# Graph network with 16 channels: TensorE gathers 28 and 31 of each super's 64 tiles, where it gathered 23 and 24

## The chip, the cores and the metric

The kernel runs on one core of a Trainium2 chip. The metric is the device time of one execution in microseconds, lower is better. The engines are TensorE (PE in the rows; PEld is its weight load), VectorE (DVE), ScalarE (ACT), GpSimd (POOL) and SyncE (SP, which only issues DMAs here).

## The reference

12500 nodes with 16 channels, 400000 edges sorted by destination. Two rounds of message passing with the same edge network, then a residual and a layer norm:

```python
w = relu(edgefeats @ fnet_w1 + fnet_b1) @ fnet_w2 + fnet_b2      # 13 -> 32 -> 16*16 per edge
W = w.reshape(-1, 16, 16)
inv_deg = 1.0 / maximum(segment_sum(ones, edge_dst), 1.0)
for _ in range(2):
    xj = hx[edge_src]                                            # gather of 16 floats per edge
    m = einsum('ei,eio->eo', xj, W)
    agg = segment_sum(m, edge_dst) * inv_deg[:, None]
    hx = gru_cell(agg, hx, ...)
out = layernorm(x + hx)
```

## The kernel before

**Tiling.** A tile is 128 edges. 64 tiles make a super, and there are 49 supers (the last one is short). A super is worked through in 8 halves `k` of 8 tiles each (`HPS = 8`, `HT = 8`). Two rounds go over all supers; between them and behind the second stand the GRU cell and the norm. Pairs of supers are the body of loops (`for_supers`); the order of instructions on each engine is the order of the code, and engines meet at semaphores.

**Two ways to gather.** The source rows of a tile, 128 rows of 16 floats, reach `xg` in one of two ways. GpSimd issues an indirect DMA for the tile (L535, waiting at each half until the products of `LEAD = 4` halves earlier are done). Or TensorE makes them: the whole node table lies in SBUF as `parts` (two parts of the floats, 125 partitions, 4 blocks of 400 columns); ScalarE builds a one-hot matrix from the tile's keys (`src_hots`: four ACTIVATE Abs at L603, one ACTIVATE Relu at L607 over all of them, for all such tiles of a half together), TensorE multiplies it with the table in 8 matmuls of 400 columns (`gather_rows`, L722: 4 blocks times 2 parts) into a PSUM bank, VectorE masks the 25 candidate rows (`pick_rows`, L1137, one instruction a tile) and sums them (`keep_rows`, L1145, one a half). `BY_PE[rnd][k]` says how many of a half's 8 tiles TensorE makes: 2, then seven times 3 in round 0 (23 of 64), eight times 3 in round 1 (24 of 64). The first super of a round is gathered by GpSimd alone. The tiles that TensorE makes in super `s` belong to super `s + 1`.

**Buffers.** `ps_g` has three PSUM banks (3, 6, 5), one for each tile of a half, and a tile waits until the same bank's last tile has been picked (`slot_free`). The first layer `hidden` (L709, round 0 only, for the next super) uses bank 2 and waits until ScalarE's relu has read it. The keys of a super are loaded by one DMA of 768 KB (L452), in a ring of two.

**TensorE's order in one half** (`emit`, L792): `products` (L732, waits for VectorE's `fan`), in round 0 `hidden`, then at `k` = 0, 2, 4, 5, 6 sums of the super before (`own_sums` L745, `aggregate` L755, `turn` L762, `scatter` L776), then `gather_rows` of the half's tiles. A fp32 matmul of the code is two MATMULs in the rows; one of the gathers is one.

**ScalarE's order**: `src_hots` of half `k + 1` stands ahead of `keep_products` (L576) and `relu` (L570) of half `k`. **VectorE's order**: `spread` (L1092), the next one-hot (L1080), `keep_hot` (L1100), sums of windows, then the picks of half `k - 1` and their sum. **SP's order** in one super: `idx`, `ef`, `keys`, `h_d` or `h_sb`, each behind its wait.

Of the kernel before, what the change touches and what calls it, by code (L numbers as in the profile page):

```python
# [10 lines left out]
ALU = mybir.AluOpType  # L11
# [21 lines left out]
BY_PE = ((2, 3, 3, 3, 3, 3, 3, 3), (3, 3, 3, 3, 3, 3, 3, 3))  # L33
# [4 lines left out]
TG = sum(GT)  # L38
PARTS = 2
# [14 lines left out]
def gnn_program(nc, x, x_t, src_tiles, src_pe_rows, src_pe_cols, dst_rows, dst_tiles, ef_t, w1_diag, w2_io, w2_oi,  # L54
# [77 lines left out]
    with ExitStack() as ctx:  # L132
# [6 lines left out]
        def sem(name):  # L139
# [31 lines left out]
        shared = sb("shared", [P, 4320 + 3 * C * AR])  # L171
# [3 lines left out]
        near_tmp, far_tmp = (shared[:, lo:lo + CHUNK * TPB] for lo in (3920, 4120))  # L175
        picked = shared[:, 4320:4320 + 3 * C * AR].rearrange("p (m c a) -> p m c a", m=3, a=AR)
# [3 lines left out]
        place = sb("place", [GROUP, 2 * BPS, SPAN])  # L180
# [5 lines left out]
        m_of, h_of = mh[:, 0:GN], mh[:, GN:2 * GN]  # L186
        h_x = sb("h_x", [P, HA])
        x_x = sb("x_x", [P, C])
        rel_x = sb("rel_x", [P, 1])
        h_xt = sb("h_xt", [HA, P])  # L190
        prod_x = sb("prod_x", [P, C, C])
        msg_x = sb("msg_x", [P, CNT + 1])
        hot_x = sb("hot_x", [P, XWIN])
        keys = sb("keys", [P, 2, TG * P], I16)
# [45 lines left out]
        ps_g = [ps_all[:, b * BANK:b * BANK + AR * C] for b in (3, 6, 5)]  # L240
# [315 lines left out]
        def _(act):  # L556
# [34 lines left out]
            def src_hots(rnd, i, par, s, k):  # L591


                buf, use = ring(rnd, i, par)
                first, some = sum(GT[:k + 1]) - BY_PE[rnd][k], BY_PE[rnd][k]
                if k == 0:
                    act.wait_ge(s_keys[buf], 16 * keys_use(rnd, i, par))
# [102 lines left out]
        def _(pe):  # L700
            pe.wait_ge(s_net, 16 * NET_LOADS)

            def hidden(rnd, i, par, sup, k):
# [734 lines left out]
```

## Time and profile before

| what | value |
|---|---|
| median of 3 runs | 5147.61 us (5144.84 to 5148.1) |
| span of the profiled execution | 6694.6 us |
| TensorE matmul busy | 5648.0 us, 84% |
| weight load busy | 4666.6 us, 70% |
| VectorE busy | 4296.9 us, 64% |
| GpSimd busy | 3811.1 us, 57% |
| ScalarE busy | 3179.0 us, 47% |
| chain that ended last | PE 65%, issue 14%, another core or an unknown queue 10%, ACT 6%, DVE 3% |

The profiled execution is 1547 us longer than the median of the runs without a profile. Its span can't be compared with the median directly. VectorE's `place<-` instruction (L1151) runs once a super, at `k = 2`, and serves as a clock of the supers.

### The profile page before, as it was taken

Reading aid. Unit: us, or ns where it says so; the run is one execution under the profiler, and the core shown is the slowest. Engines: PE = TensorE matmul, PEld = TensorE weight load, DVE = VectorE, ACT = ScalarE, POOL = GpSimd, SP = SyncE. Lnnn points to the kernel's source line nnn. Section 1 sums busy time; section 2 is a strip of 40 time slices with the busy share of each in tenths; the row PEclk is TensorE's granted clock in tenths of the full one; section 3 lists DMA queues with packets and bytes.
Section 4 is the critical chain, followed back from the end, with each engine's and each line's share of the span. In section 5 each row is a group of like instructions: output and inputs, shape, how many; then the busy total and the mean of one; then the engine's idle time right before and its main releaser. Section 6 shows DMA issues by size and latency. Waiting matters only on the chain.

```text
span 6694.6 us, 119595 instructions
## 1 busy us (share of the span) xinstructions
PE 5648.0 (84%) x38360; PEld 4666.6 (70%) x38361; DVE 4296.9 (64%) x7146; ACT 3179.0 (47%) x5259; POOL 3811.1 (57%) x4021
## 2 busy tenths in 40 slices
PE   2888888888888888888858888888888888888887
PEld 1777777777777777777647777776777777777775
DVE  3766666666666666666636666666666666666665
ACT  1554555445554545454325454454545454444442
POOL 6355555555555555555555555555555555555553
PEclk7988998889898999998878898898988889888887
DMA  4111111111111111111111111111111111111110
GB/s 107 46 34 48 34 48 34 48 34 48 34 48 44 39 48 34 48 34 48 25 47 29 40 29 40 33 37 39 31 40 29 40 29 41 29 40 29 40 29 20
DMA packets 197656, 263.32 MB, mean 39 GB/s; under 512 B 95745, under 2 KB 165942, under 8 KB 184205
## 3 DMA queue, kind: packets, MB, share of 16 engines
q1 hardware_dynamic: 61885, 216.66, 9.5%
q0 software_dynamic: 128192, 33.07, 4.8%
q10 hardware_dynamic: 7026, 6.21, 0.4%
q8 instruction: 348, 5.70, 0.4%
q14 instruction: 205, 1.68, 0.1%
HBM read 195.73 MB, written 54.92 MB: 37 GB/s over the span
## 4 chain that ended last, share of the span: by engine, by line
PE 65%; issue 14%; another core or an unknown queue 10%; ACT 6%; DVE 3%; DVEq 1%; DMA 0%; POOL 0%; ACTq 0%; POOLq 0%; SPq 0%
PE ps_all L722 45%; PE ps_all L732 8%; ACT src_hot L603 3%; PE ps_all L755 3%; PE ps_all L745 3%; PE ps_all L709 3%; PE ps_all L776 2%; ACT src_hot L607 2%; DVE shared L1137 1%; DVE fan L1092 1%; PE ps_all L762 0%; ACT shared L576 0%; ACT h_sb L570 0%; DVE xg L1145 0%
## 5 line engine op out<-in xcount | busy, mean ns | idle before, releaser
L722 PE MATMUL ps_all<-parts,src_hot 125*128 125x400 f32 x18048 | 3820.4, 368 | 258.7 <-issue 166.4
L722 PEld LDWEIGHTS ps_all<-parts,src_hot 125*128 125x128 f32 x18048 | 3501.9, 202 | 482.6 <-issue 367.7
L535 POOL DMA_INDIRECT xg<-in_x,idx x2027 | 1923.4, 949 | 1394.3 <-issue 556.1
L535 POOL DMA_INDIRECT xg<-h_rows,idx x1979 | 1873.1, 946 | 1371.6 <-issue 518.7
L1137 DVE TENSOR_TENSOR shared<-ps_all,at_hot 128x400 f32<-128x400 f32 x2256 | 1211.8, 566 | 1858.8 <-remote 1168.4
L603 ACT ACTIVATE src_hot<-keys,neg_key 128x384 fp32r<-128x384 int16 (+1 forms) x3072 | 1617.0, 599 | 1653.1 <-remote 979.0
L732 PE MATMUL ps_all<-fan,h_sb 128*32 128x160 f32 x12544 | 825.0, 316 | 489.5 <-issue 435.8
L1092 DVE TENSOR_TENSOR fan<-xg,ps_all 128x1280 f32<-128x1280 f32 x784 | 1158.8, 1478 | 88.0 <-DVE xg L1145 33.4
L607 ACT ACTIVATE src_hot<-src_hot 128x1536 fp32r<-128x1536 f32 (+1 forms) x768 | 1122.2, 1461 | 72.3 <-ACT src_hot L603 2.8
L1145 DVE TENSOR_REDUCE xg<-shared 128x48 f32<-128x1200 f32 (+1 forms) x768 | 1056.7, 1376 | 75.6 <-DVE shared L1137 1.0
L732 PEld LDWEIGHTS ps_all<-fan,h_sb 128*32 128x32 f32 x12544 | 391.8, 111 | 842.4 <-issue 794.9
L576 ACT COPY shared<-ps_all 128x320 f32<-128x320 f32 x784 | 330.2, 421 | 638.1 <-remote 431.2
L582 ACT COPY agg_sb<-ps_all 128x160 f32<-128x160 f32 x98 | 28.7, 293 | 981.0 <-remote 630.7
L755 PE MATMUL ps_all<-shared,w2s 128*64 128x160 f32 x3136 | 328.9, 349 | 70.3 <-issue 69.3
L745 PE MATMUL ps_all<-xg,shared 128*80 128x136 f32 (+1 forms) x1568 | 323.0, 317 | 75.1 <-issue 58.7
L709 PE MATMUL ps_all<-w_sb,ef 105*128 105x264 f32 x784 | 314.5, 483 | 66.5 <-issue 43.9
L745 PEld LDWEIGHTS ps_all<-xg,shared 128*80 128x80 f32 x1568 | 223.5, 168 | 193.1 <-issue 150.3
L755 PEld LDWEIGHTS ps_all<-shared,w2s 128*64 128x64 f32 x3136 | 259.3, 161 | 126.5 <-issue 117.6
L1165 DVE TENSOR_TENSOR acc_all<-acc_all,ps_all 33x144 f32 (+1 forms) x384 | 114.1, 297 | 236.3 <-remote 174.3
L709 PEld LDWEIGHTS ps_all<-w_sb,ef 105*128 105x128 f32 x784 | 131.0, 207 | 191.1 <-issue 179.4
L776 PE MATMUL ps_all<-place,agg_t 80*33 80x144 f32 (+1 forms) x1568 | 189.6, 336 | 64.0 <-issue 60.4
L1115 DVE TENSOR_TENSOR shared<-ps_all,mask 80x256 f32<-80x256 f32 (+3 forms) x490 | 180.4, 368 | 42.1 <-remote 20.4
(120 smaller groups left out, 1383.7 us busy)
## 6 DMA issues: line engine op xcount, KB each, us to landing
keys<-key_d SPq DMA_DIRECT2D x96, 768.0 KB
h_d<-h_sb SPq DMA_DIRECT2D x49, 1056.0 KB
h_sb<-h_d SPq DMA_DIRECT2D x49, 1056.0 KB
xg<-in_x,idx POOLq DMA_INDIRECT x2027
xg<-h_rows,idx POOLq DMA_INDIRECT x1979
ef<-in_ef_t SPq DMA_DIRECT2D x49, 420.0 KB
acc_all<-agg_t SPq DMA_DIRECT2D x1, 3161.0 KB
idx<-in_src_tiles SPq DMA_DIRECT2D x98, 32.0 KB
```

Source lines behind the costliest of these rows:

```text
L535: pool.indirect_dma_start(out=xg[:, buf, at, 0:C], out_offset=None, in_=rows_of, in_offset=bass.IndirectOffsetOnAxis(ap=idx[:, buf, at:at ...
L576: act.copy(pev[:, :, 2 * k:2 * k + 2, :].rearrange("p i u n -> p u i n"), ps_p[k % 2][:, 0:2 * C * WIN].rearrange("p (u i n) -> p u i n", ...
L603: act.activation(src_hot[:, k % 2, kb, 0:some * P], keys[:, buf, first * P:(first + some) * P], ACT.Abs, bias=neg_key[:, kb:kb + 1]).then_ ...
L607: act.activation(hot_of, hot_of.bitcast(F32), ACT.Relu, bias=1.0, scale=-1.0).then_inc(s_src_hot, some)
L709: pe.matmul(ps_h[:, 0:HT * HA], ef[:, buf, k, :], w1_sb[:], start=True, stop=True).then_inc(s_h, 1)
L722: last = pe.matmul(ps_g[j], src_hot[0:KP, k % 2, kb, j * P:(j + 1) * P], parts[0:KP, m, kb, :], start=(kb == 0 and m == 0), stop=(kb == KB ...
L732: last = pe.matmul(ps_p[k % 2][b * HID:(b + 1) * HID, u * C * WIN:(u + 1) * C * WIN], h_sb[:, buf, k * HT + u * BPS + b, 0:HID], fan[:, k ...
L745: last = pe.matmul(ps_own[n][:, u, 0:TQ * ca], hot_sb[:, j, b].rearrange("p t n -> p (t n)"), xg[:, buf].rearrange("p (j t b) c -> p j b t ...
L755: last = pe.matmul(ps_agg[lo:lo + BPS * C, 0:TPB * WIN], w2s[:, i, :], pev[:, i].rearrange("p t n -> p (t n)"), start=(i < 2), stop=(i >= ...
L1092: dve.tensor_tensor(fan[:, k % 2], xg[:, buf, k * HT:(k + 1) * HT, 0:C].unsqueeze(3).to_broadcast([P, HT, C, WIN]), hot[:, k % 2].unsqueez ...
L1137: dve.tensor_tensor(picked[:, j], ps_g[j].rearrange("p (a c) -> p c a", a=AR), at_hot[:, u].unsqueeze(1).to_broadcast([P, C, AR]), ALU.mul ...
L1145: dve.tensor_reduce(xg[:, buf, at:at + many, 0:C], picked[:, 0:many], AX_X, ALU.add).then_inc(s_xg_pe, many)
```

## The change

`BY_PE` becomes 3, 3, 4, 3, 3, 4, 4, 4 in round 0 (28 tiles) and 3, then seven times 4 in round 1 (31 tiles). A fourth tile of a half has its own place in `ps_g`, which is bank 2, that of the first layer. In round 0 the first layer of the next super therefore moves behind the half's first gathered tile, waits until the last fourth tile has been picked, and the fourth tile waits until the relu of this half has read the bank. Keys are loaded by two DMAs a super (halves 0 to 3 and 4 to 7, two single buffers in place of a ring of two), and the first of them stands ahead of the `idx` load in SP's queue. `place` moves into `mh`, the scratch of rare tiles and of the setup into one tile `rare`, to make room.

```diff
-BY_PE = ((2, 3, 3, 3, 3, 3, 3, 3), (3, 3, 3, 3, 3, 3, 3, 3))
+BY_PE = ((3, 3, 4, 3, 3, 4, 4, 4), (3, 4, 4, 4, 4, 4, 4, 4))
+KQ = HPS // 2
+GQ = (sum(GT[:KQ]), sum(GT[KQ:]))
...
+    def fourth_before(rnd, k):
+        back = next(b for b in range(1, HPS + 1) if BY_PE[rnd][k - b] > 3)
+        return sum(BY_PE[rnd][:k - back]) + 3 - (0 if k >= back else sum(BY_PE[rnd]))
...
-        ps_g = [ps_all[:, b * BANK:b * BANK + AR * C] for b in (3, 6, 5)]
+        ps_g = [ps_all[:, b * BANK:b * BANK + AR * C] for b in (3, 6, 5, 2)]
...
+                def keys_of(rnd, i, par, q):
+                    sup = 2 * i + par
+                    made = sum(BY_PE[rnd][:KQ * (q + 1)])
+                    wait_pos(sp, s_src_hot, pe_total(rnd) if is_first(i, par) else pe_count(rnd, sup, made))
+                    sp.dma_start(keys[:, q, 0:GQ[q] * P], ...).then_inc(s_keys[q], 16)
...
+                    if not is_last(i) and not (is_first(i, par) and rnd == 0):
+                        keys_of(rnd, i, par, 0)
                     wait_pos(sp, s_super, done)
                     sp.dma_start(idx[:, buf, :], src_tiles[bass.ds(sup * P, P), :]).then_inc(s_idx[buf], 16)
...
                     if not is_last(i):
-                        wait_pos(sp, s_src_hot, pe_total(rnd) if is_first(i, par) else pe_count(rnd, sup, 0))
-                        sp.dma_start(keys[:, 1 - buf, :], ...)
+                        keys_of(rnd, i, par, 1)
...
-            def hidden(rnd, i, par, sup, k):
+            def hidden(rnd, i, par, sup, k, s=None):
...
+                if s is not None:
+                    free = fourth_before(rnd, k)
+                    if not (isinstance(s, int) and s == 1 and free < 0):
+                        pe.wait_ge(s_picked, pe_count(rnd, s, free) + 1)
...
+                    if j == 3 and rnd == 0:
+                        pe.wait_ge(s_relu, sup * HPS + k + 1)
...
-                        if rnd == 0 and not is_last(i):
-                            hidden(rnd, i + par, 1 - par, sup + 1, k)
...
-                            gather_rows(rnd, s + 1, k)
+                            gather_rows(rnd, s + 1, k, (0,))
+                            if rnd == 0:
+                                hidden(rnd, i + par, 1 - par, sup + 1, k, s + 1)
+                            gather_rows(rnd, s + 1, k, (1, 2, 3), sup + 1)
...
-                                pick_rows(rnd, s + 1, k - 1, (2,))
+                                pick_rows(rnd, s + 1, k - 1, (2, 3))
```

TensorE, round 0, halves 5 and 6 of a super, before (L709 is the first layer, L722 the gathers, L732 the products):

```order
L732 MATMUL ps_all<-fan,h_sb 32x160 x8
L709 MATMUL ps_all<-w_sb,ef 128x264
L745 MATMUL ps_all<-xg,shared 80x136
L776 MATMUL ps_all<-place,agg_t 33x144 x4
L722 MATMUL ps_all<-parts,src_hot 128x400 x24
L732 MATMUL ps_all<-fan,h_sb 32x160 x8
L709 MATMUL ps_all<-w_sb,ef 128x264
L745 MATMUL ps_all<-xg,shared 80x136 x2
L722 MATMUL ps_all<-parts,src_hot 128x400 x24
```

The same halves in the changed kernel, where L727 is the first layer, L744 the gathers and L754 the products:

```order
L754 MATMUL ps_all<-fan,h_sb 32x160 x8
L767 MATMUL ps_all<-xg,shared 80x136
L798 MATMUL ps_all<-mh,agg_t 33x144 x4
L744 MATMUL ps_all<-parts,src_hot 128x400 x8
L727 MATMUL ps_all<-w_sb,ef 128x264
L744 MATMUL ps_all<-parts,src_hot 128x400 x24
L754 MATMUL ps_all<-fan,h_sb 32x160 x8
L767 MATMUL ps_all<-xg,shared 80x136 x2
L744 MATMUL ps_all<-parts,src_hot 128x400 x8
L727 MATMUL ps_all<-w_sb,ef 128x264
L744 MATMUL ps_all<-parts,src_hot 128x400 x24
```

Each of these halves has 32 gather matmuls in place of 24, and the first layer stands between the first 8 and the rest.

SP's queue in round 0, one super in the loop, before:

```order
L431 ISA [waits s_super]
L431 DMA idx<-in_src_tiles 128x64
L402 REGISTER_ALU
L441 ISA [waits s_h]
L441 DMA ef<-in_ef_t 105x1024
L402 REGISTER_ALU
L452 ISA [waits s_src_hot]
L452 DMA keys<-key_d 128x3072
L459 ISA [waits s_relu]
L459 DMA h_d<-h_sb 128x2112
```

And in the changed kernel:

```order
L435 ISA [waits s_src_hot]
L435 DMA keys<-key_d 128x1920
L446 ISA [waits s_super]
L446 DMA idx<-in_src_tiles 128x64
L406 REGISTER_ALU
L456 ISA [waits s_h]
L456 DMA ef<-in_ef_t 105x1024
L406 REGISTER_ALU
L435 ISA [waits s_src_hot]
L435 DMA keys<-key_d 128x2048
L473 ISA [waits s_relu]
L473 DMA h_d<-h_sb 128x2112
```

The load of the first half's keys, with a wait of its own, now stands ahead of `idx`; the second stands where the whole load stood.

## Rows read from the trace of the kernel before

**Rows 1.** VectorE's timeline, one row a super: start us, us, instruction.

```profile
215.06 1.35 DVE L1151 TENSOR_TENSOR place<-ps_all,slot_of 80x1152 f32<-80x1152 f32 x1
...
3305.59 1.34 DVE L1151 TENSOR_TENSOR place<-ps_all,slot_of 80x1152 f32<-80x1152 f32 x1
...
3528.01 1.34 DVE L1151 TENSOR_TENSOR place<-ps_all,slot_of 80x1152 f32<-80x1152 f32 x1
...
6608.58 1.34 DVE L1151 TENSOR_TENSOR place<-ps_all,slot_of 80x1152 f32<-80x1152 f32 x1
```

**Rows 2.** TensorE's timeline, round 1, halves 4 to 6 of a super.

```profile
4333.19 0.45 PE L745 MATMUL ps_all<-xg,shared 128*80 128x128 f32 x2
4333.57 0.68 PE L776 MATMUL ps_all<-place,agg_t 80*32 80x144 f32 x8
4334.18 4.64 PE L722 MATMUL ps_all<-parts,src_hot 125*128 125x400 f32 x24
4338.75 0.75 PE L732 MATMUL ps_all<-fan,h_sb 128*32 128x160 f32 x16
4339.43 0.67 PE L745 MATMUL ps_all<-xg,shared 128*80 128x128 f32 x4
4339.86 4.62 PE L722 MATMUL ps_all<-parts,src_hot 125*128 125x400 f32 x24
4344.41 0.75 PE L732 MATMUL ps_all<-fan,h_sb 128*32 128x160 f32 x16
```

**Rows 3.** TensorE's timeline, round 0: halves 2 and 3; and half 0, two tiles.

```profile
3039.63 3.19 PE L722 MATMUL ps_all<-parts,src_hot 125*128 125x400 f32 x16
3042.74 0.75 PE L732 MATMUL ps_all<-fan,h_sb 128*32 128x160 f32 x16
...
3052.79 0.71 PE L709 MATMUL ps_all<-w_sb,ef 105*128 105x264 f32 x2
3053.34 0.63 PE L745 MATMUL ps_all<-xg,shared 128*80 128x136 f32 x4
3053.81 0.43 PE L762 MATMUL ps_all<-fold,agg_sb 128*80 128x64 f32 x4
3054.05 4.62 PE L722 MATMUL ps_all<-parts,src_hot 125*128 125x400 f32 x24
...
3059.28 0.71 PE L709 MATMUL ps_all<-w_sb,ef 105*128 105x264 f32 x2
3059.63 4.54 PE L722 MATMUL ps_all<-parts,src_hot 125*128 125x400 f32 x23
```

**Rows 4.** TensorE's timeline, start of a super in round 1: single products with idle time between.

```profile
4356.23 0.47 PE L732 MATMUL ps_all<-fan,h_sb 128*32 128x160 f32 x1 [0.28 <-issue]
...
4358.68 3.03 PE L755 MATMUL ps_all<-shared,w2s 128*64 128x160 f32 x32
4361.64 4.64 PE L722 MATMUL ps_all<-parts,src_hot 125*128 125x400 f32 x24
...
5005.55 0.30 PE L732 MATMUL ps_all<-fan,h_sb 128*32 128x160 f32 x1 [1.78 <-issue]
```

**Rows 5.** GpSimd's timeline, round 1: idle time before each and what ended it.

```profile
4002.78 0.95 POOL L535 DMA_INDIRECT xg<-h_rows,idx  x1 [3.38 <-PE ps_all L732]
4004.04 0.95 POOL L535 DMA_INDIRECT xg<-h_rows,idx  x1 [0.30 <-issue]
4005.29 0.95 POOL L535 DMA_INDIRECT xg<-h_rows,idx  x1 [0.30 <-issue]
```

**Rows 6.** ScalarE's timeline, a half of two tiles and one of three.

```profile
3027.67 1.70 ACT L603 ACTIVATE src_hot<-keys,neg_key 128x256 fp32r<-128x256 int16 x4
3029.47 1.06 ACT L607 ACTIVATE src_hot<-src_hot 128x1024 fp32r<-128x1024 f32 x1
...
3042.32 2.13 ACT L603 ACTIVATE src_hot<-keys,neg_key 128x384 fp32r<-128x384 int16 x4
3044.54 1.48 ACT L607 ACTIVATE src_hot<-src_hot 128x1536 fp32r<-128x1536 f32 x1
```

**Rows 7.** VectorE, busy time and counts of two stretches of 47 supers (windows; PE, PEld, DVE, ACT, POOL in turn).

```profile
215.00:3305.60 3090.60, 2706.68 (x18535) 2248.69 (x18538) 2016.41 (x3351) 1559.30 (x2703) 1807.00 (x1911) 0.91 0.16 41
3528.00:6608.60 3080.60, 2653.66 (x18166) 2218.86 (x18168) 2041.91 (x3377) 1489.93 (x2332) 1773.21 (x1876) 0.88 0.13 35
```

More of the change, by code:

```diff
@@ L107, in landed @@
         return i * (16 * usual) + 16 * (earlier + usual + first + last)
-    def keys_use(rnd, i, par):
-        buf, use = ring(rnd, i, par)
-        return use - sum(ring(r, 0, 0)[0] == buf for r in range(rnd + 1))
     def pe_total(rnd):
@@ L170, in gnn_program @@
         fan = sb("fan", [P, 2, HT, C, WIN])
-        shared = sb("shared", [P, 4320 + 3 * C * AR])
+        shared = sb("shared", [P, 3920 + max(GT) * C * AR])
         pev = shared[:, 0:C * TPB * WIN].rearrange("p (i t n) -> p i t n", i=C, n=WIN)
@@ L174, in gnn_program @@
         own = shared[0:GROUP, 3640:3640 + 2 * CA * TQ]
-        near_tmp, far_tmp = (shared[:, lo:lo + CHUNK * TPB] for lo in (3920, 4120))
-        picked = shared[:, 4320:4320 + 3 * C * AR].rearrange("p (m c a) -> p m c a", m=3, a=AR)
+        picked = shared[:, 3920:3920 + max(GT) * C * AR].rearrange("p (m c a) -> p m c a", m=max(GT), a=AR)
         agg_sb = sb("agg_sb", [P, TPB * WIN])
@@ L179, in gnn_program @@
         slot_of = sb("slot_of", [GROUP, NSUP * 2 * BPS])
-        place = sb("place", [GROUP, 2 * BPS, SPAN])
         acc_all = sb("acc_all", [P, N + SPAN])
@@ L186, in gnn_program @@
         m_of, h_of = mh[:, 0:GN], mh[:, GN:2 * GN]
+        place = mh[0:GROUP, 0:2 * BPS * SPAN].rearrange("g (b n) -> g b n", n=SPAN)
         h_x = sb("h_x", [P, HA])
@@ L189, in gnn_program @@
         rel_x = sb("rel_x", [P, 1])
-        h_xt = sb("h_xt", [HA, P])
-        prod_x = sb("prod_x", [P, C, C])
+        rare = sb("rare", [P, WC + XWIN + P])
+        prod_x = rare[:, 0:WC].rearrange("p (o i) -> p o i", o=C)
+        hot_x = rare[:, WC:WC + XWIN]
+        h_xt = rare[0:HA, WC + XWIN:WC + XWIN + P]
+        near_tmp, far_tmp = (rare[:, lo:lo + CHUNK * TPB] for lo in (0, CHUNK * TPB))
         msg_x = sb("msg_x", [P, CNT + 1])
-        hot_x = sb("hot_x", [P, XWIN])
-        keys = sb("keys", [P, 2, TG * P], I16)
+        keys = sb("keys", [P, 2, max(GQ) * P], I16)
         at_pe = sb("at_pe", [P, NSUP * TG])
@@ L425, in _ @@
             for rnd in range(ROUNDS):
+                def keys_of(rnd, i, par, q):
+                    sup = 2 * i + par
+                    made = sum(BY_PE[rnd][:KQ * (q + 1)])
+                    wait_pos(sp, s_src_hot, pe_total(rnd) if is_first(i, par) else pe_count(rnd, sup, made))
+                    sp.dma_start(keys[:, q, 0:GQ[q] * P],
+                                 key_d[bass.ds(sup + 1, 1), sum(GQ[:q]) * P:sum(GQ[:q + 1]) * P].to_broadcast(
+                                     [P, GQ[q] * P])).then_inc(s_keys[q], 16)
                 def emit(i, par, rnd=rnd):
@@ L449, in emit @@
                         sp.wait_ge(s_key_d, 16)
+                    if is_first(i, par) and rnd == 0:
+                        keys_of(rnd, i, par, 0)
                     if not is_last(i):
-                        wait_pos(sp, s_src_hot, pe_total(rnd) if is_first(i, par) else pe_count(rnd, sup, 0))
-                        sp.dma_start(keys[:, 1 - buf, :],
-                                     key_d[bass.ds(sup + 1, 1), :].to_broadcast([P, TG * P])).then_inc(
-                                         s_keys[1 - buf], 16)
+                        keys_of(rnd, i, par, 1)
                     if rnd == 0 and isinstance(i, int) and i == 0 and par == 1:
@@ L591, in src_hots @@
             def src_hots(rnd, i, par, s, k):
[L594 to L597, printed above, removed]
+                q = k // KQ
+                first, some = sum(GT[KQ * q:k + 1]) - BY_PE[rnd][k], BY_PE[rnd][k]
+                if k % KQ == 0:
+                    act.wait_ge(s_keys[q], 16 * (rnd * (NSUP - 1) + s))
                 if k > 1:
@@ L602, in src_hots @@
                 for kb in range(KB):
-                    act.activation(src_hot[:, k % 2, kb, 0:some * P], keys[:, buf, first * P:(first + some) * P],
+                    act.activation(src_hot[:, k % 2, kb, 0:some * P], keys[:, q, first * P:(first + some) * P],
                                    ACT.Abs, bias=neg_key[:, kb:kb + 1]).then_inc(s_src_far, 1)
@@ L708, in hidden, with gather_rows @@
                 wait_pos(pe, s_relu, sup * HPS + k)
+                if s is not None:
+                    free = fourth_before(rnd, k)
+                    if not (isinstance(s, int) and s == 1 and free < 0):
+                        pe.wait_ge(s_picked, pe_count(rnd, s, free) + 1)
                 pe.matmul(ps_h[:, 0:HT * HA], ef[:, buf, k, :], w1_sb[:],
                           start=True, stop=True).then_inc(s_h, 1)
-            def gather_rows(rnd, s, k):
+            def gather_rows(rnd, s, k, js, sup=None):
                 for j, (n, _, _) in enumerate(pe_tiles(rnd, k)):
+                    if j not in js:
+                        continue
                     pe.wait_ge(s_src_hot, pe_count(rnd, s, n) + 1)
+                    if j == 3 and rnd == 0:
+                        pe.wait_ge(s_relu, sup * HPS + k + 1)
                     if isinstance(s, int) and s == 1 and slot_free(rnd, k, j) < 0:
@@ L844, in emit @@
                                     pe.wait_ge(s_ht_x, tiles_x)
-                                    pe.matmul(ps_x[:, P:P + WC], h_xt[:], w2_sb[:],
+                                    pe.matmul(ps_x[:, P:P + WC], h_xt, w2_sb[:],
                                               start=True, stop=True).then_inc(s_w_x, 1)
@@ L849, in emit @@
                                         pe.wait_ge(s_hot_x, sums_x)
-                                        pe.matmul(ps_x[0:CNT + 1, P + WC:P + WC + XWIN], msg_x[:], hot_x[:],
+                                        pe.matmul(ps_x[0:CNT + 1, P + WC:P + WC + XWIN], msg_x[:], hot_x,
                                                   start=True, stop=True).then_inc(s_sum_x, 1)
@@ L1150, in places @@
                 wait_pos(dve, s_sc, 2 * sup)
-                dve.tensor_tensor(place[:], iota_ps[0:GROUP].unsqueeze(1).to_broadcast([GROUP, 2 * BPS, SPAN]),
+                dve.tensor_tensor(place, iota_ps[0:GROUP].unsqueeze(1).to_broadcast([GROUP, 2 * BPS, SPAN]),
                                   slot_of[:, bass.ds(s * 2 * BPS, 2 * BPS)].unsqueeze(2).to_broadcast(
@@ L1241, in emit @@
                                     dve.wait_ge(s_turn_x, tiles_x)
-                                    dve.tensor_copy(h_xt[:], ps_x[0:HA, 0:P])
+                                    dve.tensor_copy(h_xt, ps_x[0:HA, 0:P])
                                     dve.drain().then_inc(s_ht_x, 1)
@@ L1254, in emit @@
                                         dve.drain()
-                                        dve.tensor_tensor(hot_x[:], iota[:, 0:XWIN],
+                                        dve.tensor_tensor(hot_x, iota[:, 0:XWIN],
                                                           rel_x[:].to_broadcast([P, XWIN]), ALU.is_equal)
```

8 lines of the change are left out of this document (4 added, 4 removed).

## The prediction

> **What bounds the kernel now.** I read the clock of the supers first. Between the `place` rows of the first and the 48th super lie 3305.6 - 215.1 = 3090.5 us in round 0 and 6608.6 - 3528.0 = 3080.6 us in round 1 [rows 1]: 47 supers each, 65.8 and 65.5 us a super. Everything else (setup, the first super of a round, GRU, norm) is 6694.6 - 6171.1 = 523.5 us.
>
> Then I put this against the median, 5147.6 us. If the 523.5 us are the same without a profile, a pair of supers (one of each round) takes (5147.6 - 523.5) / 47 = 98.4 us there, against 131.3 in the trace. So the trace holds some 33 us a pair that the timed runs don't have. TensorE's timeline shows where: at the start of supers, and once more inside them, products run one by one with 0.28 to 1.8 us idle before each, ended by "issue" [rows 4], while in clean stretches all 16 take 0.68 us together [rows 2]. The durations inside clean stretches are what I build on, not the gaps.
>
> TensorE's work of a super, from start to start in clean stretches:
> - gathers of three tiles: 4338.75 - 4334.18 = 4.57 and 4344.41 - 4339.86 = 4.55 us [rows 2]; of two, 3.11 us [rows 3]. One more tile is 1.45 us (8 matmuls of 181 ns).
> - products 0.68 us a half, 5.4 us a super [rows 2]
> - own sums 0.38 us ahead of each of two scatters, 0.43 once [rows 2], 0.47 twice [rows 3]: 2.1 us; scatters 2 x 0.61 = 1.2 us [rows 2]; turn 0.24 us [rows 3]; aggregate 4361.64 - 4358.68 = 2.96 us [rows 4]
> - first layer, round 0 only: 0.55 us in the five halves where sums follow, 0.35 us in three [rows 3]: 3.8 us
>
> Round 1: 8 x 4.56 + 12.0 = 48.5 us. Round 0: 7 x 4.56 + 3.11 + 12.0 + 3.8 = 50.8 us. A pair is 99.3 us, and 523.5 + 47 x 99.3 = 5191 us, 0.8% above the median. So **TensorE, without a gap, accounts for the whole time**. GpSimd accounts for it nearly as well: one indirect DMA starts every 1.25 us [rows 5], 41 and 40 a super are 51.3 and 50.0 us, 101.3 us a pair, 3% above the 98.4. Both engines are full, and in the trace it is GpSimd that waits, for L732 [rows 5].
>
> **The change part by part.**
>
> *Five and seven more tiles on TensorE.* 12 x 1.45 = 17.4 us a pair. Nothing hides it: it stands in TensorE's own queue. 47 x 17.4 = **818 us**. Round 0 is then 58.1 us, round 1 58.7 us, a pair 116.7 us.
>
> *Five and seven fewer on GpSimd.* 36 and 33 a super: 45.0 and 41.3 us. It leaves the path and gives nothing while TensorE needs 58 us. In the first super of a round GpSimd still makes all 64 tiles, 80 us, and covers TensorE's extra tiles there, so 47 supers pay, not 48.
>
> *ScalarE.* Going from two to three tiles, the four Abs go from 1.70 to 2.13 us and the Relu from 1.06 to 1.48 us [rows 6], so four tiles are about 2.56 + 1.90 us, with copy and relu some 5.3 us a half, beside TensorE's 6.0 + 0.7 us or more. Hidden, except at half 1 of a super: its one-hots are only begun when ScalarE has copied the aggregate and the products, and TensorE has by then only one half's gathers and a product ahead. In round 1 half 1 gets a fourth tile, 0.85 us more there; between 0 (slack takes it) and 0.85 x 47 = 40 us. I take 19 us.
>
> *VectorE.* It is busy 2016 / 47 = 42.9 and 2042 / 47 = 43.4 us a super [rows 7]. A tile adds one pick and a third of a three-tile sum, about 1.0 us: 48 and 51 us, under 58. The longer `at_hot` adds 0.2. Hidden; if TensorE's tile were cheaper, this would be the next bound.
>
> *The first layer between gathers, round 0.* Its matmuls are the same. But the gathers are cut once more: 24 matmuls at 181 ns are 4.35 us, the row is 4.56, so each run of gathers has a 0.2 us edge. Eight more edges a super in round 0: 0 (the edge of the first layer may have been paid before) to 8 x 0.19 x 47 = 71 us; I take half, 36 us. Its new wait, the last fourth tile picked, is met: VectorE picks it about 0.6 us after the gather ends, TensorE comes there after products and a tile, over 2 us later. The fourth tile's wait for the relu is closer. ScalarE is free 4.5 us after the last gather ended, plus 0.8 us: 5.3 us; TensorE arrives after 0.68 + 3 x 1.45 + 0.35 = 5.4 us. At worst some 0.3 us in four halves, within the range.
>
> *Keys in two loads, the first ahead of `idx`.* The same bytes and one more issue a super. SP now holds `idx` back until the one-hots of half 3 are made, about when TensorE is in half 2 or 3; behind it are queued `ef`, the second keys and `h_d` or `h_sb`. GpSimd wants `idx` at half 4, and has 58 - 45 = 13 us of slack. The first keys are needed again some four halves later, 28 us. I cost it at nothing; if the cover is gone, one half (7 us) every super, 650 us, which nothing in the order points to. `place` and the scratch move without new work.
>
> Sum against the median: 5147.6 + 818 + 36 + 19 = **6020 us**. A profiled execution has gaps on top: 6694.6 + 870, about 7570 us.
>
> One rule speaks against this. Rows 2 show 4.57 us for 24 matmuls of 400 columns, 190 ns each with the edge. The Trainium skill, TensorE: Matmul & The Clock Gate, "Back-to-back issue gap", gives a stream of weight load and matmul pairs about 81 ns a matmul at 128 columns and 131 at 512. An estimate from that page is 116 ns at 400 columns, a tile 0.93 us, and by it TensorE's pair of supers would be about 86 us and the change would pay: that is the last rival below with the page's price. The trace does not agree with it.
>
> **The rivals.**
>
> *Cheaper gathers than traced, slower all the same: about 5675 us.* A matmul of 400 columns at 2.4 GHz can't take under 167 ns; 181 is 14 more, and those could be the profile's. A tile would be 1.33 us, the pair 116.7 - 59 x 0.12 = 109.6 us, 523.5 + 47 x 109.6 = 5675 us. Before, GpSimd would then have been the bound. For it: both engines account for the median. Against it: 181 ns is steady through every clean run, also right behind idle time.
>
> *A ring of waits takes over: about 6175 us.* Gather, pick, bank free, gather; or relu late for the fourth tile. 0.3 us in each of the 11 four-tile halves of a pair is 47 x 3.3 = 155 us more. For it: ScalarE's 5.3 against 5.4 us. Against: VectorE has 7 us of slack a super.
>
> *The other side, faster: GpSimd is the bound and TensorE has much air in timed runs.* If the issue gaps are the visible part of a slowing that touches every TensorE instruction in the profile, the clean rows overstate it. GpSimd then takes 98.4 / 81 = 1.215 us a tile, and 69 tiles a pair instead of 81 give 83.8 us: 523.5 + 47 x 83.8 = 4460 us at the most favourable, 4460 to 5137 in all. It decides from the point where TensorE's 116.7 us are really under 98.4, 16% less than the rows. Against it: 59 tiles at the columns' own 1.33 us are already 78.7 us, which leaves 19.7 us for edges and work that the rows put at 31. By the page's figure it would come to about 4580 us.
>
> *The change doesn't do what it says*: excluded, the order shows 32 matmuls where 24 stood.
>
> **How the numbers follow.** TensorE full as traced 0.53 (6020, own range 5950 to 6090); cheaper gathers 0.19; ring of waits 0.09; faster 0.16; within 0.2%, which is about what a measurement of this kernel can tell from no change, 0.03. Slower is 0.81. The range 5500 to 6180 us holds the first, nearly all of the second and most of the third, 0.8.
>
> **What would show it.** The changed kernel's clean stretches should show 32 gather matmuls in 6.0 us, the round-0 first layer between 8 and 16 or 24 of them, and GpSimd waiting for L754 in nearly every half, 10 us or more a super. Supers should be 8 us longer in round 0 and 10 in round 1 than before. Wrong would be: gathers at under 170 ns, or GpSimd without waits for the products; and a time near or under 5150 us would say that TensorE was not the bound at all.

## The result and the profile after

| | before | after |
|---|---|---|
| median | 5146.26 us (5144.84 to 5148.1, 4 runs) | 5905.53 us (5902.23 to 5906.21, 4 runs) |
| span of the profiled execution | 6694.6 us | 5904.2 us |

The ratio is 1.1476, 95% interval 1.1462 to 1.149: the change makes the kernel 759 us slower. The profiled execution of the changed kernel is as long as its timed ones. That of the kernel before was 1548 us longer than its timed ones. The experiments show that such a difference goes with the chip that the program runs on; the chip of that first profile isn't on record.

The page of the changed kernel, busy time and what ended most of the idle time (groups: count, busy us, mean ns, idle us before and what ended most of it):

```profile
PE 5698.3 (97%) x42968; PEld 5092.0 (86%) x42969; DVE 4856.4 (82%) x7722; ACT 3663.0 (62%) x5259; POOL 3261.6 (55%) x3445
...
L744 PE MATMUL ps_all<-parts,src_hot 125*128 125x400 f32 x22656 | 4467.0, 351 | 30.1 <-ACT src_hot L621 23.2
...
L549 POOL DMA_INDIRECT xg<-in_x,idx x1787 | 1696.2, 949 | 1211.2 <-PE ps_all L754 739.1
L549 POOL DMA_INDIRECT xg<-h_rows,idx x1643 | 1550.8, 944 | 1324.9 <-PE ps_all L754 920.3
```

TensorE is 97% busy. GpSimd, with 576 indirect DMAs fewer, waits for the products 1659 us in all, and TensorE waits for ScalarE's one-hots only 23 us. TensorE's timeline in round 1, halves 3 to 5, the pendant of [rows 2]:

```profile
4020.82 0.75 PE L754 MATMUL ps_all<-fan,h_sb 128*32 128x160 f32 x16
4021.50 6.10 PE L744 MATMUL ps_all<-parts,src_hot 125*128 125x400 f32 x32
4027.53 0.75 PE L754 MATMUL ps_all<-fan,h_sb 128*32 128x160 f32 x16
4028.21 0.45 PE L767 MATMUL ps_all<-xg,shared 128*80 128x128 f32 x2
4028.59 0.69 PE L798 MATMUL ps_all<-mh,agg_t 80*32 80x144 f32 x8
4029.20 6.09 PE L744 MATMUL ps_all<-parts,src_hot 125*128 125x400 f32 x32
4035.23 0.75 PE L754 MATMUL ps_all<-fan,h_sb 128*32 128x160 f32 x16
```

Four tiles take 4027.53 - 4021.50 = 6.03 us, 1.46 us more than the 4.57 of three [rows 2], with nothing between the groups. Round 0, one half with the first layer inside the gathers, between its products and the next ones, the pendant of [rows 3]:

```profile
2010.60 0.75 PE L754 MATMUL ps_all<-fan,h_sb 128*32 128x160 f32 x16
2011.28 1.72 PE L744 MATMUL ps_all<-parts,src_hot 125*128 125x400 f32 x8
2012.84 0.61 PE L727 MATMUL ps_all<-w_sb,ef 105*128 105x264 f32 x2
2013.09 4.72 PE L744 MATMUL ps_all<-parts,src_hot 125*128 125x400 f32 x24
2017.73 0.75 PE L754 MATMUL ps_all<-fan,h_sb 128*32 128x160 f32 x16
```

The clock of the supers, VectorE's `place` instruction (now in `mh`, L1174), as in [rows 1]:

```profile
174.13 1.35 DVE L1174 TENSOR_TENSOR mh<-ps_all,slot_of 80x1152 f32<-80x1152 f32 x1
...
2898.61 1.34 DVE L1174 TENSOR_TENSOR mh<-ps_all,slot_of 80x1152 f32<-80x1152 f32 x1
...
3084.08 1.34 DVE L1174 TENSOR_TENSOR mh<-ps_all,slot_of 80x1152 f32<-80x1152 f32 x1
...
5825.98 1.34 DVE L1174 TENSOR_TENSOR mh<-ps_all,slot_of 80x1152 f32<-80x1152 f32 x1
```

47 supers take 2724.5 and 2741.9 us: 57.97 and 58.34 us each, 116.3 a pair. The forecast had 58.1 and 58.7 plus 1.2 for edges and waits.

### The profile page after: what moved, and what is told of

It is laid out like the page before. It is cut to its first block, busy times and chain, and to the rows that moved or that the text cites. A ratio compares the mean times of both kernels' runs of the same rounds, so it can differ in the third digit from the quotient of the medians.

```text
span 5904.2 us, 131764 instructions
## 1 busy us (share of the span) xinstructions
PE 5698.3 (97%) x42968; PEld 5092.0 (86%) x42969; DVE 4856.4 (82%) x7722; ACT 3663.0 (62%) x5259; POOL 3261.6 (55%) x3445
## 4 chain that ended last, share of the span: by engine, by line
PE 89%; ACT 3%; issue 3%; DVE 2%; DMA 2%; POOL 1%; DVEq 0%; SPq 0%; POOLq 0%; ACTq 0%
PE ps_all L744 67%; PE ps_all L754 8%; PE ps_all L767 4%; PE ps_all L777 4%; PE ps_all L727 3%; PE ps_all L798 2%; ACT src_hot L617 2%; POOL xg L549 1%; ACT src_hot L621 1%; DMA acc_all<-agg_t 1%; PE ps_all L784 0%; DMA h_sb<-h_d 0%; PE ps_all L930 0%; DVE fan L1115 0%; DVE shared L1160 0%
## 5 line engine op out<-in xcount | busy, mean ns | idle before, releaser
L744 PE MATMUL ps_all<-parts,src_hot 125*128 125x400 f32 x22656 | 4467.0, 351 | 30.1 <-ACT src_hot L621 23.2
L744 PEld LDWEIGHTS ps_all<-parts,src_hot 125*128 125x128 f32 x22656 | 4084.4, 188 | 198.9 <-issue 116.4
L617 ACT ACTIVATE src_hot<-keys,neg_key 128x512 fp32r<-128x512 int16 (+1 forms) x3072 | 1862.5, 678 | 1016.2 <-PE ps_all L744 1004.0
L549 POOL DMA_INDIRECT xg<-in_x,idx x1787 | 1696.2, 949 | 1211.2 <-PE ps_all L754 739.1
L549 POOL DMA_INDIRECT xg<-h_rows,idx x1643 | 1550.8, 944 | 1324.9 <-PE ps_all L754 920.3
L1160 DVE TENSOR_TENSOR shared<-ps_all,at_hot 128x400 f32<-128x400 f32 x2832 | 1527.0, 566 | 674.5 <-PE ps_all L744 656.5
L621 ACT ACTIVATE src_hot<-src_hot 128x2048 fp32r<-128x2048 f32 (+1 forms) x768 | 1369.8, 1784 | 70.5
L1168 DVE TENSOR_REDUCE xg<-shared 128x64 f32<-128x1600 f32 (+1 forms) x768 | 1297.3, 1689 | 81.1 <-DVE shared L1160 2.4
L754 PE MATMUL ps_all<-fan,h_sb 128*32 128x160 f32 x12544 | 599.4, 309 | 115.2 <-DVE fan L1115 103.8
L754 PEld LDWEIGHTS ps_all<-fan,h_sb 128*32 128x32 f32 x12544 | 331.5, 110 | 335.3 <-issue 283.7
L727 PE MATMUL ps_all<-w_sb,ef 105*128 105x264 f32 x784 | 244.1, 392 | 30.9 <-DMA ef<-in_ef_t 18.8
L777 PEld LDWEIGHTS ps_all<-shared,w2s 128*64 128x64 f32 x3136 | 213.3, 141 | 19.5 <-issue 17.4
L1103 DVE TENSOR_TENSOR ps_all<-ps_all,rel 128x80 f32<-128x80 f32 x784 | 189.3, 241 | 0.2 <-DVE ps_all L1092 0.2
```

What stands on the lines that cost most here:

```text
L549: pool.indirect_dma_start(out=xg[:, buf, at, 0:C], out_offset=None, in_=rows_of, in_offset=bass.IndirectOffsetOnAxis(ap=idx[:, buf, at:at ...
L617: act.activation(src_hot[:, k % 2, kb, 0:some * P], keys[:, q, first * P:(first + some) * P], ACT.Abs, bias=neg_key[:, kb:kb + 1]).then_in ...
L621: act.activation(hot_of, hot_of.bitcast(F32), ACT.Relu, bias=1.0, scale=-1.0).then_inc(s_src_hot, some)
L727: pe.matmul(ps_h[:, 0:HT * HA], ef[:, buf, k, :], w1_sb[:], start=True, stop=True).then_inc(s_h, 1)
L744: last = pe.matmul(ps_g[j], src_hot[0:KP, k % 2, kb, j * P:(j + 1) * P], parts[0:KP, m, kb, :], start=(kb == 0 and m == 0), stop=(kb == KB ...
L754: last = pe.matmul(ps_p[k % 2][b * HID:(b + 1) * HID, u * C * WIN:(u + 1) * C * WIN], h_sb[:, buf, k * HT + u * BPS + b, 0:HID], fan[:, k ...
```

## The experiments

Three jobs ran on chips where the kernel before takes 5145 us, two on chips where the same program takes 6712 and 6742 us in all its runs. I call them chips without gaps and with gaps. A time below is compared only with the kernel before of its own job.

**1. The kernel before again.** No edit.

> The kernel before, unchanged, profiled once more. Its first profiled execution was 6694.6 us long against 5146 us timed, with idle time ended by issue in front of TensorE's small matmuls; the changed kernel's profiled execution (5904.2 us) had none. If the profile of this kernel makes the gaps, the span is 6600 to 6800 us again and the time 5146. If they were an accident of that one execution, the span is about 5145 us, the supers are about 50.1 us each, and GpSimd's waits for the products can be read.

Measured: 6737.75 us; the kernel before took 6742.34 us there (19 timed runs, 6695 to 6774), profiled span 6744.8. Neither expectation was met in full: the gaps are neither the profile's nor an accident, and on this chip the kernel takes 1600 us more, timed or profiled. TensorE's timeline there:

```profile
4299.23 0.31 PE L732 MATMUL ps_all<-fan,h_sb 128*32 128x160 f32 x1 [0.98 <-issue]
4299.95 0.30 PE L732 MATMUL ps_all<-fan,h_sb 128*32 128x160 f32 x1 [0.41 <-issue]
4301.35 0.47 PE L732 MATMUL ps_all<-fan,h_sb 128*32 128x160 f32 x2 [1.11 <-issue]
4302.07 0.43 PE L732 MATMUL ps_all<-fan,h_sb 128*32 128x160 f32 x1 [0.24 <-issue]
4303.47 0.76 PE L732 MATMUL ps_all<-fan,h_sb 128*32 128x160 f32 x3 [0.97 <-issue]
```

The starts are 0.72 and 1.40 us apart where sixteen should take 0.68 us, and no semaphore ends the waits.

The granted clock of TensorE belongs to this picture: its mean is 0.880 here and 0.981 in experiment 9, on a chip without gaps. When the burst above begins the clock is still full (1.00 up to 4300 us); from 4302 to 4308 us it is at its lower level (0.50, 1.2 GHz), and the 24 gather matmuls behind the burst take 5.45 us in place of 4.57. Over the whole run the clock is at the lower level for 1616 us in 176 stretches, against 199 us in 22 stretches in experiment 9; 148 of the 176 begin within 3 us of such a gap. So the 1587 us between the two profiles (6744.8 - 5158.0) are idle time and low clock together: TensorE's matmuls are busy 5653.5 us here and 4914.0 us there, for the same 38360 instructions.

**2. The structure of the change with the old table.**

```diff
-BY_PE = ((3, 3, 4, 3, 3, 4, 4, 4), (3, 4, 4, 4, 4, 4, 4, 4))
+BY_PE = ((2, 3, 3, 3, 3, 3, 3, 3), (3, 3, 3, 3, 3, 3, 3, 3))
```

> The changed kernel with the table of before (23 and 24 tiles): keys in two halves ahead of idx, the first layer behind the first gathered tile, scratch moved; the tile counts alone undone. If the tiles on TensorE are the whole cost, as forecast, the time is 5146 us plus the forecast's edges of 36 us at most, 5130 to 5185. If the keys ahead of idx or the moved first layer cost something of their own, it is 5200 or more, and the tiles cost less than 1.45 us each.

Beside the table, `fourth_before` returns nothing when a round has no fourth tile, and `shared` keeps its size. The waits between the first layer and the fourth tile are therefore absent here.

Measured: 6720.72 us against 6742.34, ratio 0.9977 (0.9953 to 1.0001), on the chip with gaps. The structure alone costs nothing visible there. For a chip without gaps it says little, as what bounds the kernel isn't the same.

**3 and 4. Half of the gather matmuls.** Both kernels leave out the low part of the nodes in the gathers, so their gathered rows are rounded.

```diff
-                        for m in range(PARTS):
+                        for m in range(1):
...
-                                             start=(kb == 0 and m == 0), stop=(kb == KB - 1 and m == PARTS - 1))
+                                             start=(kb == 0 and m == 0), stop=(kb == KB - 1))
```

> The kernel before with the low part of the nodes left out of the gathers (4 matmuls a tile in place of 8, so the gathered rows are rounded). TensorE's pair of supers falls from about 98.3 us in clean rows to 98.3 - 47 x 0.73 = 64 us. If GpSimd sets the time of the kernel before (81 tiles x 1.25 us = 101.3 us a pair), nothing is gained: 5100 to 5146 us. If TensorE sets it and GpSimd has air, the time falls by a good part of the 34 us a pair: under 4800 us.

> The changed kernel with the low part of the nodes left out of the gathers (4 matmuls a tile in place of 8). TensorE's pair falls from 116.3 to about 116.3 - 59 x 0.73 = 73 us. What is next then sets the time: GpSimd's 69 tiles x 1.25 = 86.3 us a pair give about 438 + 47 x 86.3 = 4490 us; VectorE's 48 + 51 us busy give about 5090 us. Either way far under 5905: the added matmuls are the cost.

Measured, on the chip with gaps: 6440.24 us (ratio 0.9549) and 5978.44 us (ratio 0.8853), the kernel before at 6742.34. Half of the gather matmuls gone gives 302 us in the kernel before, though 18048 / 2 matmuls at 181 ns are 1633 us. That isn't the price of the matmuls on such a chip: the mean granted clock fell with them, from 0.880 in experiment 1 to 0.786, and a gather matmul's mean duration rose from 370 to 415 ns. The expectations were made for a chip without gaps, so they stay untested, and so does the question of the bound there; experiments 7, 9 and 10 settle it.

**5. The changed kernel again.** No edit; a chip without gaps.

> The changed kernel, unchanged. In the runs before this one the kernel before took 6742 us on its chip, with the issue gaps of its first profile, timed or profiled alike, so the gaps come with the chip and not with the profile. If this chip is free of them, the kernel before takes 5146 us and this one 5905. If it has them, the kernel before takes 6742 us. Theory 1 (the gaps come after runs of small matmuls that empty TensorE's queue, and longer gathers refill it): this one is then slower by less than on the good chip, 6742 plus 0 to 400 us. Theory 2 (a fixed loss of some 15 us a super): 6742 + 760 = 7500 us.

Measured: 5903.81 us against 5144.58, ratio 1.1478 (1.1459 to 1.1497): the result repeats.

**6. A table between the two**, on the structure of the change (here too `fourth_before` may return nothing, which doesn't come up with this table):

```diff
-BY_PE = ((3, 3, 4, 3, 3, 4, 4, 4), (3, 4, 4, 4, 4, 4, 4, 4))
+BY_PE = ((3, 3, 3, 3, 3, 3, 4, 3), (3, 3, 4, 3, 3, 4, 3, 3))
```

> The changed kernel with 25 and 26 tiles a super on TensorE, between the two tables. On a chip without gaps TensorE is full from 98.3 us a pair on: 98.3 + 4 x 1.45 = 104.1 us a pair, 438 + 47 x 104.1 = 5331 us. If GpSimd set the time of the kernel before, with TensorE having air, it is below 5146. On a chip with gaps: between the two kernels' own times there.

Measured: 5400.39 us against 5144.58, ratio 1.0497 (1.048 to 1.0515). Slower than both expectations, with 25 and 26 tiles; supers of 53.7 and 51.9 us. Three and five tiles of 1.45 us fewer than 57.97 and 58.34 would be 53.6 and 51.1: round 0 is as the tiles say, round 1 0.8 us over. The trace has these 0.8 us (waiting line, waited for: us in total, times, longest us):

```profile
PE ps_all L756 <- DMA h_sb<-h_d: 35.6, 43, 1.6
```

35.6 us over 47 supers are 0.76 us each. TensorE waits for the nodes' load, which stands behind the second key load in SP's queue. With the kernel before (experiments 9 and 10) this wait doesn't appear, and in the changed kernel's profile it is 1.3 us in all. So with shorter supers the new order of the loads seems to have a price; no run with the old order and this table shows it apart.

**7. Fewer tiles on TensorE**, on the kernel before:

```diff
-BY_PE = ((2, 3, 3, 3, 3, 3, 3, 3), (3, 3, 3, 3, 3, 3, 3, 3))
+BY_PE = ((2, 3, 2, 3, 3, 2, 3, 3), (3, 3, 2, 3, 3, 2, 3, 3))
```

> The kernel before with 21 and 22 tiles a super on TensorE in place of 23 and 24. On a chip without gaps: if GpSimd sets the time of the kernel before (1.25 us a tile), a pair is 85 x 1.25 = 106.3 us and the time 438 + 47 x 106.3 = 5430 us, some 5 us per super slower. If TensorE sets it alone and GpSimd has air, 4 x 1.45 us less a pair: 5146 - 270 = 4876 us. On a chip with gaps GpSimd waits for TensorE, so fewer tiles are faster or the same, 6500 to 6742 us.

Measured: 5385.35 us against 5144.58, ratio 1.0467 (1.0449 to 1.0484). Fewer tiles are slower: GpSimd sets the time. The waits of this kernel (engine, line, waited for: us in total, times, longest us):

```profile
DVE fan L1092 <- DMA xg<-h_rows,idx: 504.1, 271, 17.8
DVE fan L1092 <- DMA xg<-in_x,idx: 485.9, 236, 5.7
...
POOL xg L535 <- PE ps_all L732: 48.8, 160, 0.3
```

VectorE waits 990 us for landings of the indirect DMAs, and GpSimd waits for nobody: 160 waits of at most 0.3 us are the usual pause between two DMAs. The 5385 us are 45 under the expected 5430.

**8. The first layer ahead of the first gathered tile**, on the changed kernel, round 0:

```diff
-                            gather_rows(rnd, s + 1, k, (0,))
                             if rnd == 0:
                                 hidden(rnd, i + par, 1 - par, sup + 1, k, s + 1)
+                            gather_rows(rnd, s + 1, k, (0,))
```

> The changed kernel with the first layer ahead of the half's first gathered tile in round 0, as before the change; it still waits for the last fourth tile's pick. The forecast put 0 to 71 us on the cut of the gathers, 36 taken. The rows of the changed kernel put it at nothing: the two edges of a cut half are 0.17 us each more, the first layer's own time 0.25 us in place of 0.35 to 0.55. So by the forecast it is 36 us faster than 5905 on a chip without gaps, by the rows within 10 us; slower by more than 30 us if the earlier place makes TensorE wait for VectorE's pick of the fourth tile.

Measured: 5892.63 us, 11 us under the 5903.81 of the same job. Between the two expectations, nearer to the rows.

**9. The kernel before on a chip without gaps.** No edit.

> The kernel before once more, for its profile on a chip without gaps. With 21 and 22 tiles GpSimd issued an indirect DMA every 1.249 us through both rounds without a pause, and 4198 x 1.249 us plus 138 us around them are its 5384 us. The kernel before has 4006: 4006 x 1.249 + 138 = 5141 us. If GpSimd sets its time, the profile shows it waiting for the products for less than 50 us in all and the products waiting for fan. If TensorE sets it (47 pairs x 98.3 us in clean rows plus about 438 around them: 5058 us), GpSimd waits for the products in most halves. On a chip with gaps: 6742 us, as there.

Measured: 5144.94 us, ratio 1.0; profiled span 5158.0. The waits:

```profile
DVE fan L1092 <- DMA xg<-h_rows,idx: 293.0, 181, 17.4
...
POOL xg L535 <- PE ps_all L732: 67.5, 210, 2.3
```

GpSimd's timeline there, and TensorE's a little later:

```profile
4004.83 0.94 POOL L535 DMA_INDIRECT xg<-h_rows,idx  x1 [0.30 <-PE ps_all L732]
4006.08 0.95 POOL L535 DMA_INDIRECT xg<-h_rows,idx  x1 [0.30 <-issue]
```

```profile
4005.15 2.39 PE L755 MATMUL ps_all<-shared,w2s 128*64 128x160 f32 x32
4007.47 4.64 PE L722 MATMUL ps_all<-parts,src_hot 125*128 125x400 f32 x24
4012.86 0.75 PE L732 MATMUL ps_all<-fan,h_sb 128*32 128x160 f32 x16 [0.75 <-DVE fan L1092]
...
4031.28 4.64 PE L722 MATMUL ps_all<-parts,src_hot 125*128 125x400 f32 x24
4036.73 0.75 PE L732 MATMUL ps_all<-fan,h_sb 128*32 128x160 f32 x16 [0.80 <-DVE fan L1092]
```

GpSimd's waits put down to the products, 67.5 us in 210 times, are mostly the usual 0.3 us between two DMAs (210 x 0.3 = 63). It keeps its 1.25 us, and TensorE is the one that waits, 0.75 and 0.80 us for `fan`. The clock of the supers:

```profile
128.48 1.35 DVE L1151 TENSOR_TENSOR place<-ps_all,slot_of 80x1152 f32<-80x1152 f32 x1
...
2529.17 1.34 DVE L1151 TENSOR_TENSOR place<-ps_all,slot_of 80x1152 f32<-80x1152 f32 x1
...
2719.72 1.34 DVE L1151 TENSOR_TENSOR place<-ps_all,slot_of 80x1152 f32<-80x1152 f32 x1
...
5067.49 1.34 DVE L1151 TENSOR_TENSOR place<-ps_all,slot_of 80x1152 f32<-80x1152 f32 x1
```

2400.7 and 2347.8 us for 47 supers are 51.08 and 49.95 us a super; 41 and 40 DMAs at 1.249 us are 51.2 and 50.0. In these stretches GpSimd issues 1916 and 1877 indirect DMAs, 1.251 us apart in the mean; only 9 and none of them start more than 1.3 us after the one before. The kernel before runs at GpSimd's pace.

**10. One tile more than before.**

```diff
-BY_PE = ((2, 3, 3, 3, 3, 3, 3, 3), (3, 3, 3, 3, 3, 3, 3, 3))
+BY_PE = ((3, 3, 3, 3, 3, 3, 3, 3), (3, 3, 3, 3, 3, 3, 3, 3))
```

> The kernel before with 24 tiles in both rounds, three in every half. If GpSimd sets the time, 48 indirect DMAs fewer are 48 x 1.249 = 60 us off it, and TensorE gets 48 x 1.45 = 70 us more: 438 + 47 x 99.8 = 5129 us is its own sum, GpSimd's is 5081. So 5129 us or a little under 5144 if the two meet there; 5190 or more if TensorE was the bound before.

Measured: 5194.34 us against 5145.35, ratio 1.0097 (1.008 to 1.0114). The expectation of 5129 was wrong, and by its number 5190 should mean that TensorE was the bound before. Experiments 7 and 9 exclude that. Round 0 went from 51.1 to 52.1 us a super where GpSimd's 40 DMAs need 50.0: with the 24th tile TensorE has crossed over. The 5129 us rested on a sum of clean rows of 50.1 us for 23 tiles, so 51.55 for 24, about 0.5 us under the 52.1 measured. In round 0 the bounds meet between 23 and 24 tiles; in round 1, which has no first layer, 24 tiles (49.8 us) are still at GpSimd's pace.

Supers by tiles on TensorE, chips without gaps, from the clock of the supers of each profile:

| tiles, round 0 | us a super | tiles, round 1 | us a super |
|---|---|---|---|
| 21 | 53.5 | 22 | 52.4 |
| 23 (before) | 51.1 | 24 (before) | 50.0 |
| 24 | 52.1 | 24 | 49.8 |
| 25 | 53.7 | 26 | 51.9 |
| 28 (after) | 58.0 | 31 (after) | 58.3 |

**11. Key loads behind the setup loads, once.** In the changed kernel's SP queue, for the second super of round 0 alone:

```diff
-                    if not is_last(i) and not (is_first(i, par) and rnd == 0):
+                    second = rnd == 0 and isinstance(i, int) and i == 0 and par == 1
+                    if not is_last(i) and not (is_first(i, par) and rnd == 0) and not second:
                         keys_of(rnd, i, par, 0)
...
-                    if not is_last(i):
+                    if not is_last(i) and not second:
                         keys_of(rnd, i, par, 1)
...
+                    if second:
+                        keys_of(rnd, i, par, 0)
+                        keys_of(rnd, i, par, 1)
```

> The changed kernel with one move in SP's queue: in the second super of round 0 both key loads stand behind the setup loads (meta, slot_of, the zeroing of the sums) and the h_d store, where they stood ahead of them. In the changed kernel's profile those setup loads wait for the one-hots of half 7 (100.9 us in place of 40.4), and TensorE then sits idle 42 us once for fan. Theory: the clock of the supers starts some 45 us earlier and the time is 5860 us, supers unchanged at 58.0 and 58.2. Rival: the idle time is GpSimd's or the late idx load, and the time stays at 5900.

What it was to explain, in the changed kernel's profile, SP's and TensorE's timelines:

```profile
72.94 0.43 SPq L446 DMA_DIRECT2D idx<-in_src_tiles  x1
...
100.53 0.33 SPq L435 DMA_DIRECT2D keys<-key_d  x1
100.90 0.42 SPq L414 DMA_DIRECT2D shift_d<-perm  x1
...
113.17 17.51 SPq L479 DMA_DIRECT2D acc_all<-agg_t  x2
```

```profile
106.21 4.72 PE L744 MATMUL ps_all<-parts,src_hot 125*128 125x400 f32 x24
153.06 1.29 PE L754 MATMUL ps_all<-fan,h_sb 128*32 128x160 f32 x16 [42.12 <-DVE fan L1115]
```

Measured: 6228.17 us; this job fell on a chip with gaps, where the kernel before took 6711.83: ratio 0.928 (0.9252 to 0.9308). The first `place` came at 214.4 us, against 251.4 us in experiment 12 with the loads in the change's order:

```profile
214.39 1.35 DVE L1178 TENSOR_TENSOR mh<-ps_all,slot_of 80x1152 f32<-80x1152 f32 x1
```

```profile
251.42 1.35 DVE L1176 TENSOR_TENSOR mh<-ps_all,slot_of 80x1152 f32<-80x1152 f32 x1
```

So the move gives back 37 us at the start, in the same job, though with another table. The kernel before has its first `place` at 214.8 us on such a chip (experiment 1), so nothing of the delay is left. The expected 5860 us and the 45 us on a chip without gaps weren't tried.

The larger finding is the ratio. On a chip with gaps the new table (with this move) makes the kernel 7% faster, 484 us, where on the others the change makes it 15% slower. The mean granted clock is 0.967 in this run, against 0.885 in experiment 12.

**12. The structure with the old table again.** The kernel of experiment 2.

> The changed kernel with the table of before (23 and 24 tiles), run before only on the chip with gaps. On a chip without gaps GpSimd's 4006 x 1.249 us are the bound again, and the supers are as before the change, 51.1 and 50.0 us. Left is the late setup, 45 us once: 5190 us. If the keys ahead of idx cost something in every super, 5240 or more; if the late setup hides beside GpSimd's first 105 tiles, 5145. On a chip with gaps, 6720 as before.

Measured: 6696.05 us against 6711.83, ratio 0.996 (0.9938 to 0.9982), on the chip with gaps. With experiment 11 this puts the 7% on the table: the same structure with the old table gives 0.4%. The time of the structure alone on a chip without gaps stays unmeasured. The table above bounds it in round 0: from 24 tiles without the structure to 25 with it, a super grows by 53.7 - 52.1 = 1.7 us (53.73 and 52.07 unrounded), of which a tile is 1.45; about 0.2 us a super, some 10 us in all, is left for it. That is the size of what experiment 8 gives back.

## Why the prediction was right, and where it wasn't

The forecast, slower and 6020 us, was 115 us over 5905.5, inside its range. Between the profiles of experiment 9 and of the changed kernel the spans differ by 746 us: 323.8 in 47 supers of round 0 (2724.5 - 2400.7), 394.1 in those of round 1 (2741.9 - 2347.8), 28 elsewhere.

*TensorE's price of a tile: right, its sum right with some luck.* 1.46 us measured, 1.45 forecast; the pair 116.3 us against 116.7 from the rows of before. The aggregate in this sum is 1.3 us a pair too long (below). Against it stand 45 us in which TensorE is idle in the 47 pairs (5466.5 us less 5421.2 busy), 1.0 us a pair. The forecast "10 us or more of waits a super on GpSimd" holds: 1659 / 98 = 17 us.

*"TensorE, without a gap, accounts for the whole time": wrong.* It was GpSimd, at 51.08 + 49.95 = 101.0 us a pair. The forecast saw both engines as full and took the wrong one. Two numbers from a profile with gaps misled it. The 523.5 us around the supers are 409.5 us in experiment 9 (5158.0 - 4748.5), which makes the pair 2.6 us longer than the 98.4 computed, and right at GpSimd's 101.3. And the aggregate of 2.96 us [rows 4] stood behind a burst of gaps, at a mean granted clock of 0.77; it takes 4007.47 - 4005.15 = 2.32 us in experiment 9, so TensorE's own sum was 99.3 - 1.3 = 98.0 us a pair, 3 us under what the kernel takes. That GpSimd waited for L732 in [rows 5] was true only of such a chip.

*The term of 818 us was therefore too large.* The first tiles filled air that TensorE had. The steady supers pay 717.9 us: 116.3 - 101.0 = 15.3 us a pair in place of 17.4.

*The gaps are the profile's: wrong.* They belong to the chip. The forecast kept to the durations in clean stretches and left the gaps out, and on the chips that timed the change there were none, so the number survived. For a chip with gaps no forecast was made; by experiment 11 its sign would have been wrong, though the change without that move was not run there. "About 7570 us" for the profiled execution fell with it: 5904.2.

*The first layer between gathers, 36 us (0 to 71): the size was wrong.* A cut half has the edge twice, but the layer itself takes 0.25 us (2013.09 - 2012.84) in place of 0.35 to 0.55 [rows 3]. Experiment 8 puts the place at 11 us in all.

*ScalarE at half 1, 19 us: the size near, the place wrong.* TensorE waits 23.2 us for the one-hots in the whole run, in the page above, against 7.9 us in experiment 9. But the 47 waits are 0.49 us at half 1 in round 0, which has three tiles before and after. In round 1, where the forecast put them because half 1 gets its fourth tile, there are none. So that the number fits is luck.

*Keys ahead of `idx`, costed at nothing: right in the steady supers of this table, wrong once.* The slack of four halves exists only when the loop runs. In the second super the two key loads wait for one-hots of halves 3 and 7, and behind them stood not only `idx`, `ef` and `h_d`, which the forecast named, but the setup loads, which it didn't. The sums' zeroing went out at 113 us, and TensorE idled 42 us once. The clock of the supers starts at 174.1 in place of 128.5 us; 17 us come back between and behind the rounds.

*The rivals.* Cheaper gathers (5675 us) is refuted in its premise, 400 columns still take 181 ns; its other half, GpSimd bound before, was true. The ring of waits did not come: VectorE waits 656.5 us for the gathers, TensorE 1.8 us for VectorE's picks. The faster side failed where it was said to decide: the pair is 116.3 us, not under 98.4. The rate of matmuls in the page "TensorE: Matmul & The Clock Gate" of the Trainium skill, "Back-to-back issue gap", 131 ns at 512 columns, is not reached: 32 matmuls of 400 columns take 6.03 us, 188 ns each with the edge.

## What to carry to other kernels

When two engines share a job by a table, measure the pace of each alone (here 1.25 us a tile on GpSimd, 1.46 on TensorE plus the rest of its queue) and find the crossing with one table on either side: 21 and 22 tiles (too much for GpSimd) were 4.7% slower, 24 in both rounds (too much for TensorE in round 0) 1.0%. A load put ahead in an in-order DMA queue has to be checked in the first iterations, where the slack of the loop does not exist. And when a profiled execution is much longer than the timed ones, run the program again before calling the difference the profile's: a table can be the faster one on one chip and the slower one on another. Look at the granted clock of each run as well: where it falls with an experiment's edit, as in experiment 3, the time saved is not the price of what was taken out.

## What the runs showed of the hardware

The same program took 5145 us on two chips, 8 and 12, and 6712 to 6742 us on two others, 2 and 7, each steady within 1.2%. On the latter TensorE's small matmuls start 0.7 or 1.4 us apart in bursts, about 11 such starts a super, with no semaphore behind them, and the granted clock falls from full to 0.50 mostly right behind such a gap (148 of 176 times in experiment 1). TensorE is not alone in it: VectorE's picks (L1137) wait 152.3 us in experiment 1 for nothing that the profile shows, and 9.2 us in experiment 9. The profile's instruction transfers of 16 KB (348 in both) are hardly slower there, 1.04 us in the median against 1.00.

Of pairs of neighbouring TensorE instructions 0.66 to 0.74 us apart there were 971 in experiment 1, 864 in experiment 12 and 62 in experiment 11, which has the new table; in experiment 9 there were 11. It is tempting to say that gathers of 32 matmuls in place of 24 refill a queue that the small matmuls empty. Experiment 4 speaks against it: with the new table and half of its gather matmuls, at most 16 in a half, there were 211, and in experiment 3, the old table with 12 at most, 699. So the gaps go with the table more than with the length of the gathers. Why, and why two chips differ, stays open, and so does what the plain change takes on a chip with gaps.
